# A deformable-convolution kernel on one core: output rows taken in pairs, bands of four pixels, masks copied into PSUM

## The reference, cut to what matters

```python
value = (xf @ vp_w.T + vp_b).reshape(n, L, G, cg)          # G = 8 groups of 8 channels
om = depthwise3x3(x) .reshape(n, L, c) @ om_w.T + om_b     # per group: 9 taps x (dy, dx, mask)
...
sampled = bilinear sample of value at (base + off), 4 neighbours each
out = jnp.einsum('nhwgk,nhwgkc->nhwgc', mask, sampled)
out = out.reshape(n, L, c) @ op_w.T
```

## Time and profile before

| | |
|---|---|
| median of 3 runs | 2954.0 us (2952.28 to 2957.7) |
| profiled execution | 2952.3 us, which is its span too |
| TensorE busy | 2707.7 us, 92% of the span |
| weight loads (beside it) | 2151.1 us, 73% |
| VectorE | 2190.7 us, 74% |
| ScalarE | 2106.7 us, 71% |
| GpSimd | 1925.4 us, 65% |

### The profile page before, as it was taken

The page is one execution under the profiler, slowest core; times in us unless marked ns, Lnnn a source line. Parts: engine busy times, 40 slices in busy tenths (PEclk is TensorE's granted clock), DMA queues, the critical chain, the costliest instruction groups (busy, mean ns, idle before and its releaser), DMA issues. The chain is left out here.

```text
span 2952.3 us, 99348 instructions
## 1 busy us (share of the span) xinstructions
PE 2707.7 (92%) x40456; PEld 2151.1 (73%) x40456; DVE 2190.7 (74%) x3095; ACT 2106.7 (71%) x4273; POOL 1925.4 (65%) x1451
## 2 busy tenths in 40 slices
PE   3999789993899999999999999999999999999998
PEld 2666456772677778787778777777878787777886
DVE  3555423334989898988889797989798888989763
ACT  2444256653887878787878787787878787878782
POOL 1000000003888988888888888888988888888892
PEclk8999889996899999999999999999999999999999
DMA  4555579974677777777777786777777777777675
GB/s 106 129 127 151 131 203 265 266 192 155 163 188 198 204 202 196 191 214 194 206 194 205 186 216 186 197 204 191 208 192 214 187 205 191 205 192 213 170 182 153
DMA packets 343610, 559.00 MB, mean 189 GB/s; under 512 B 159184, under 2 KB 245712, under 8 KB 342992
## 3 DMA queue, kind: packets, MB, share of 16 engines
q1 hardware_dynamic: 284112, 461.96, 62.0%
q10 hardware_dynamic: 59136, 91.76, 8.8%
HBM read 351.36 MB, written 202.19 MB: 187 GB/s over the span
## 5 line engine op out<-in xcount | busy, mean ns | idle before, releaser
L1273 PE MATMUL acc_p<-abuf,vbd 128*32 128x170 f32 (+9 forms) x20480 | 1033.8, 371 | 10.4 <-issue 9.6
L1273 PEld LDWEIGHTS acc_p<-abuf,vbd 128*32 128x32 f32 (+1 forms) x20480 | 805.1, 144 | 230.6 <-issue 24.9
L1106 ACT ACTIVATE dwt<-xp,wts 128x224 f32<-128x224 f32 x2016 | 803.3, 487 | 41.0 <-ACT wst L1130 32.3
L977 DVE TENSOR_TENSOR pr<-mh_p,ht 128x864 f32<-128x864 f32 x672 | 668.9, 1051 | 23.2
L1250 PE MATMUL win_p<-pr,smat 128*128 128x160 f32 x4032 | 617.0, 308 | 13.2 <-POOL pr L1063 12.2
L243 PE MATMUL cv<-cin,wb 128*64 128x392 bf16 x6912 | 590.1, 333 | 26.0 <-ACT cin L222 26.0
L1250 PEld LDWEIGHTS win_p<-pr,smat 128*128 128x128 f32 x4032 | 562.6, 192 | 39.1 <-issue 13.7
L243 PEld LDWEIGHTS cv<-cin,wb 128*64 128x64 bf16 x6912 | 401.7, 110 | 208.3 <-ACT cin L222 26.1
L1046 POOL TENSOR_TENSOR dwt<-dwt 128x896 f32<-128x896 f32 x224 | 519.1, 2317 | 4.7 <-ACT dwt L1106 4.7
L1060 POOL TENSOR_TENSOR pr<-pr 128x576 f32<-128x576 f32 x224 | 316.6, 1413 | 211.4 <-DVE pr L977 211.4
L967 DVE TENSOR_TENSOR mh_p<-oms,ht 128x864 f32<-128x864 f32 x224 | 392.3, 1752 | 7.1 <-ACT ht L1121 7.1
(11 more groups left out here) (131 smaller groups left out, 2579.7 us busy)
## 6 DMA issues: line engine op xcount, KB each, us to landing
abuf<-weight_scratch SPq DMA_DIRECT2D x784, 240.0 KB, 4.1
weight_scratch<-wst ACTq DMA_DIRECT2D x112, 800.0 KB, 5.1
xt<-x SPq DMA_DIRECT2D x128, 392.0 KB, 7.5
rows_scratch<-vsb SPq DMA_DIRECT2D x224, 128.0 KB, 3.2
vbd<-rows_scratch SPq DMA_DIRECT2D x896, 32.0 KB, 4.5
x_scratch<-xt SPq DMA_DIRECT2D x64, 392.0 KB, 6.7
y<-x SPq DMA_DIRECT2D x64, 392.0 KB, 5.4
x3h<-x_scratch SPq DMA_DIRECT2D x64, 392.0 KB, 5.7
```

Of the source, the lines that this page charges most:

```text
L977: dve.tensor_tensor(pr[:, j % 2, slots, :, :, :].rearrange("p k e x z -> p e k (x z)"), mh[:, a, :, :].rearrange("p (k x) z -> p k (x z)", ...
L1106: ins = act.activation(dwt[:, j % 2, k, :].rearrange("p (r w) -> p r w", w=W), image[:, r:r + BR, k % 3:k % 3 + W], ACT.Identity, scale=dw ...
L1273: mm = pe.matmul(acc_p[32 * (2 * s + b):32 * (2 * s + b) + 32, 0:2 * TN].rearrange("p (k w) -> p k w", w=W)[:, k0:k1 + 1, x0:x1], vbd[0:K, ...
```

## The change

Four things are edited. A cell grows from five to six rows of numbers (RP = 6) and its numbers are laid out so that those of two neighbouring output rows are neighbours; the contraction takes output rows in pairs (two neighbouring numbers of each cell), 48 rows of a block where it took 40, and its PSUM tile has the two rows interleaved, which `copy_acc` undoes. Bands are read for four pixels at a time: 14 reads of 16 partitions and 96 KB for 7 of 32 and 240 KB; a band as written is 960 KB for 800. `copy_weights` makes four copies of 200 numbers for two of 480 and 320. And `copy_om` is split: offsets to SBUF first in the step, masks after the products straight into the middle part of the mask products' PSUM tile; `mask_hats` multiplies the outer two parts from there (one instruction), waits, and multiplies the middle in place. `hj` is dropped, its copy goes to a part of `ht`, which ScalarE writes again later, after a wait (`far_ok`).

```diff
-PC = 2 * BR * RT * 2
+RP = RT + 1
+WP = 172
+PC = 2 * BR * RP * 2
 BAND = CT * PC
-LINE = GS * 12 * PC + PC
-SEEN = 12 * PC
+PX = 4
+SEEN = (PX + CT - 1) * PC
+LINE = GS * SEEN + PC
...
-        READS = (4, 3)
+        READS = (32 // PX, 24 // PX)
...
-                    for b in range(4 * half, 4 * half + READS[half]):
...
-                        sp.dma_start(abuf[32 * m:32 * m + 32, :, at:at + SEEN], seen).then_inc(a_in[half], 16)
+                    for m in range(READS[half]):
...
+                        sp.dma_start(abuf[GS * PX * m:GS * PX * (m + 1), :, at:at + SEEN], seen).then_inc(a_in[half], 16)
...
+                def offset_sums(i, j, to, lo, hi):
+                    return dve.tensor_tensor(
+                        to.rearrange("q w (b k g) -> q (w b) k g", b=2, g=GS),
+                        om_p[:, :].rearrange("q (k z) -> q k z", k=BR)[:, :, G * lo:G * hi].rearrange("q k (v g) -> q v k g", g=GS),
+                        ombt[:, G * lo:G * hi].rearrange("q (v g) -> q v g", g=GS).unsqueeze(2).broadcast_to(
+                            [LANES, 2 * (hi - lo), BR, GS]), ALU.add)
+                def copy_offsets(i, j):
+                    dve.wait_ge(om_ready, NT * i + j + 1)
+                    offset_sums(i, j, oms[:, j % 2, :, :], 0, 2 * TAPS).then_inc(off_ok, 1)
+                def copy_masks(i, j):
+                    t = NT * i + j
+                    dve.wait_ge(om_ready, t + 1)
+                    wait(dve, pr_ok, 3 * t)
+                    offset_sums(i, j, mh[:, 1, :, :], 2 * TAPS, 3 * TAPS).then_inc(om_ok, 1)
                 def mask_hats(i, j):
-                    wait(dve, pr_ok, 3 * (NT * i + j))
-                    dve.wait_ge(hat_ok, NT * i + j + 1)
-                    dve.tensor_tensor(mh[:, :, :, :],
-                                      oms[:, j % 2, 2 * TAPS:3 * TAPS, :].unsqueeze(1).broadcast_to([LANES, 3, TAPS, BR * G]),
-                                      ht[:, j % 2, :, 0:TAPS, :], ALU.mult).then_inc(mh_ok, 1)
+                    t = NT * i + j
+                    dve.wait_ge(om_ok, t + 1)
+                    dve.wait_ge(hat_ok, t + 1)
+                    dve.tensor_tensor(mh[:, 0:3:2, :, :], mh[:, 1, :, :].unsqueeze(1).broadcast_to([LANES, 2, TAPS, BR * G]),
+                                      ht[:, j % 2, 0:3:2, 0:TAPS, :], ALU.mult).then_inc(outer_ok, 1)
+                    dve.wait_ge(outer_ok, t + 1)
+                    dve.tensor_tensor(mh[:, 1, :, :], mh[:, 1, :, :], ht[:, j % 2, 1, 0:TAPS, :], ALU.mult).then_inc(mh_ok, 1)
...
                     if n:
-                        copy_om(*n)
+                        copy_offsets(*n)
                     n = near(i, j, 1, first, last)
                     if n:
                         mask_hats(*n)
                         products(*n)
+                    n = near(i, j, 2, first, last)
+                    if n:
+                        copy_masks(*n)
...
+                pool.memset(wst[:, :, :], 0.0)
                 pool.memset(abuf[:, :, :], 0.0).then_inc(band_clear, 1)
...
-                    act.activation(hj[:, :, :], ht[:, u, 1, :, :], ACT.Relu, bias=minus1[:, :], accum_out=far[:, bass.ts(t, 1)])
+                    act.activation(ht[:, u, 0, :, :], ht[:, u, 1, :, :], ACT.Relu, bias=minus1[:, :], accum_out=far[:, bass.ts(t, 1)]).then_inc(far_ok, 1)
                     act.activation(ht[:, u, 1, :, :], ht[:, u, 1, :, :], ACT.Identity, scale=-1.0, bias=1.0)
+                    act.wait_ge(far_ok, t + 1)
                     act.activation(ht[:, u, 0, :, :], off, ACT.Relu, scale=-1.0).then_inc(hat_ok, 1)
...
-                    for h, cells in ((0, 3), (1, 2)):
-                        m, at = RT * cells, BANK * h
+                    for k in range(BR):
+                        to = 2 * BR * (2 - 2 * (k % 2)) + BR * u + k
+                        cells = wst[:, 0, to:to + 1]
                         ins = act.activation(
...
+                            bass.AP(cells.tensor, cells.offset, [cells.ap[0], [PC, CT], [2 * BR, 2 * RT], [BAND, GS]]),
+                            win_p[:, 0:CT * WP].rearrange("p (e z) -> p e z", e=CT)[:, :, 0:RT * BR * G].rearrange(
+                                "p e (m k g) -> p e m k g", k=BR, g=GS)[:, :, :, k, :],
+                            ACT.Copy)
...
-                        k0, k1 = max(0, yq - y0 - 2), min(2 * BR - 1, yq - y0 + 2)
+                        t0, t1 = max(0, yq - y0 - 2) // 2, min(2 * BR - 1, yq - y0 + 2) // 2
...
-                                mov = bass.AP(seen.tensor, seen.offset + at, [seen.ap[0], [4 * BR + 2, n], [PC, x1 - x0]])
+                                mov = bass.AP(seen.tensor, seen.offset + at, [seen.ap[0], [8 * BR + 2, t1 - t0 + 1], [PC, x1 - x0], [1, 2]])
```

More of the change, by code:

```diff
@@ L787, in l1_pass @@
         tap_ok, dw1_ok, dw2_ok, dw3_ok, dw_ok = map(sem, ("tap_ok", "dw1_ok", "dw2_ok", "dw3_ok", "dw_ok"))
-        om_ready, om_ok, abs_ok, hat_ok, mh_ok, pr_ok, mg1_ok, mg_ok = map(sem, (
-            "om_ready", "om_ok", "abs_ok", "hat_ok", "mh_ok", "pr_ok", "mg1_ok", "mg_ok"))
+        om_ready, off_ok, om_ok, outer_ok, abs_ok, far_ok, hat_ok, mh_ok, pr_ok, mg1_ok, mg_ok = map(sem, (
+            "om_ready", "off_ok", "om_ok", "outer_ok", "abs_ok", "far_ok", "hat_ok", "mh_ok", "pr_ok", "mg1_ok", "mg_ok"))
         win_ok, wst_ok, amat_ok, accs_ok, misc_ready, misc_ok, carried, passed = map(sem, (
@@ L850, in read_weights @@
                     lines = w_d[D % 2, :]
-                    for b in range(4 * half, 4 * half + READS[half]):
-                        m = b % 4
-                        seen = bass.AP(lines.tensor, lines.offset + 8 * b * LINE, [[SEEN, 32], [XL * LINE, S], [1, SEEN]])
-                        at = (QB * half + 8 * m) * PC
-                        sp.dma_start(abuf[32 * m:32 * m + 32, :, at:at + SEEN], seen).then_inc(a_in[half], 16)
+                    for m in range(READS[half]):
+                        seen = bass.AP(lines.tensor, lines.offset + (32 * half + PX * m) * LINE,
+                                       [[SEEN, GS * PX], [XL * LINE, S], [1, SEEN]])
+                        at = (QB * half + PX * m) * PC
+                        sp.dma_start(abuf[GS * PX * m:GS * PX * (m + 1), :, at:at + SEEN], seen).then_inc(a_in[half], 16)
                 def write_values(i, j):
@@ L954, in copy_values @@
                     return ins
-                def copy_om(i, j):
-                    dve.wait_ge(om_ready, NT * i + j + 1)
[L958 to L962, removed]
@@ L1017, in _ @@
                     read_misc(j + 1, value=(0, j))
-                for j in range(2):
-                    copy_om(0, j)
+                copy_offsets(0, 0)
+                copy_masks(0, 0)
+                copy_offsets(0, 1)
                 mask_hats(0, 0)
                 products(0, 0)
+                copy_masks(0, 1)
                 for j in range(NT):
@@ L1112, in hats @@
                     t, u = NT * i + j, j % 2
-                    off = oms[:, u, 0:2 * TAPS, :]
+                    off = oms[:, u, :, :]
                     wait(act, pr_ok, 3 * (t - 1))
-                    act.wait_ge(om_ok, t + 1)
+                    act.wait_ge(off_ok, t + 1)
                     act.activation(ht[:, u, 1, :, :], off, ACT.Abs).then_inc(abs_ok, 1)
@@ L1149, in copy_acc @@
                     act.wait_ge(amat_ok, 2 * (D + 1))
-                    act.activation(accs[:, :, :].rearrange("p u f -> p (u f)"), acc_p[:, 0:2 * TN], ACT.Copy).then_inc(accs_ok, 1)
+                    act.activation(accs[:, :, :].rearrange("p u (k r w) -> p (u k) r w", r=2, w=W),
+                                   acc_p[:, 0:2 * TN].rearrange("p (t w r) -> p t r w", t=BR, r=2), ACT.Copy).then_inc(accs_ok, 1)
                 def step(i, j, first, last):
@@ L1247, in windows @@
                         terms = [(a, b) for a in range(3) for b in range(3) if 2 - (a + b - 2) == e]
-                        to = BANK * (e // 3) + 160 * (e % 3)
+                        to = WP * e
                         for n, (a, b) in enumerate(terms):
```

10 lines of the change are left out of this document (3 added, 7 removed).

## The result

| | before | after |
|---|---|---|
| median of the runs | 2953.6 us (2952.28 to 2957.7) | 2968.9 us (2964.83 to 2969.92) |
| ratio | | 1.0048, 95% interval 1.0035 to 1.0061 |
| profiled execution | 2952.3 us | 2968.0 us |
| mean of a pair, 15 pairs | 137.1 us | 137.9 us |
| mean granted clock | 0.97 | 0.95 |

What follows compares the result with a forecast made beforehand. VectorE was taken to bound steps with a half-piece sum and TensorE plain steps. From 2952.3 us, -70 for shorter steps and +33 for the clock gave 2915 profiled, 2917 median; range 2860 to 3000, the forecast's own 2880 to 2945.

Steps and rivals of the forecast that it cites:

- the ring: TensorE's next block waits for VectorE's late mask copy, and VectorE for TensorE's projection: 8.89 us a plain step.
- plain step: Step without a half-piece sum (4, 9 to 13), ending on TensorE before; forecast at 8.89 us, set by the mask-copy wait.
- rival 4: VectorE's in-place mask products in PSUM run at half rate, 0.9 us more a step: 3073 us, chance 0.06.
- sum steps: Six steps with one half-piece sum on VectorE, which waits for GpSimd's merges; forecast at 9.2 us each.
- Contraction: TensorE's matmuls reading two neighbouring numbers: 3.07 and 2.35 us forecast, from 5.28 and 4.14, at 0.94 ns a column.
- rival 3: Pairs in TensorE's contraction are read no faster, so its step takes 10.3 us: 3115 us, chance 0.10.
- rival 1: Gaps slow TensorE's clock, so every step's block runs at 1.2 GHz: 2982 us, chance 0.19.
- rival 2: ScalarE, with dearer weight copies, sets the step at 9.0 us and more: 2955 us, no difference, chance 0.10.
- 133.2 against 137.5: Forecast us for a pair of samples (14 steps) against today's: -4.3 a pair, -65 us over 15 pairs.
- steps 7 and 8: Heavy step 7 forecast at 14.1 us; step 8, which loses most by waiting for the mask copy, at 10.5.
- the clock: TensorE's half-clock stretches after longer gaps, charged in one step of three: +33 us, of 98 if in all.
- Costed at nothing: ScalarE's four copies, SP's extra reads, DMA landing times, values and loads, and GpSimd's extra memset: no time added.

Runs made afterwards that it cites:

- half_reads: The changed kernel with only the first half of the band reads, 7 for 14 in two steps, other pixels left zero: 2911.1 us, ratio 0.9863.
- spread: The changed kernel with TensorE's windows placed between two halves of the contraction, same instructions: 2943.7 us, ratio 0.9965 to the kernel before.
- spread_loads_first: The changed kernel with the contraction split around the windows, and all loads put ahead of the band reads in their step: 2935.1 us, ratio 0.9933.
- more_code: The changed kernel with 12 more matmuls of one number each behind the windows of every step: 2972.6 us, ratio 1.0077 to the kernel before.
- bands_of_8: The changed kernel with bands read for eight pixels at a time, half the reads but one and a half times the bytes: 3011.3 us, ratio 1.0201.

## Why the prediction was wrong

Right, by its own steps:
- **VectorE and the ring.** The plain step above, and the two mask products at 754 and 466 ns in place in PSUM: rival 4 falls. Of the plain steps a fifth stay under 8.88 us (8.89 forecast), of the sum steps under 9.11 (9.2).
- **Contraction.** Pairs are read faster, so rival 3 falls: 3.38 and 2.79 us for 5.28 and 4.14. They were forecast at 3.07 and 2.35; the difference of 0.4 us stays within the ring. A column took 1.04 ns (3.38 / 3264) for 1.94. The rule of the Trainium skill that was weighed there ("SBUF — State Buffer", the note on cachelines under "Door 1: The DMA port swizzle") agrees: one number of a line is dear, and two neighbours come near the rate of long runs.
- **Rivals 1 and 2.** ScalarE's copies came out at the upper bound: four of 200 take 1.68 us a step and two took 0.89. ScalarE still waits for offsets (116 us after), so it does not hold the ring. A block at half clock in every step (rival 1) is not there: the block with its projection took over 2.5 us in 30 of 215 steps after, 7 of 216 before, and the forecast had charged one in three. Stretches at 0.50 in L1 did grow, from 44 to 171 us in all. Rival 1's 2982 and rival 2's 2955 lie nearest to 2968.9 by luck: neither one's mechanism sets the steps.

Wrong: **the sum, "133.2 against 137.5", and what was added to it**. The sum set steps built from clean rows against the mean of six real pairs, which holds delays of its own. Taken alike, as the times which a fifth of each of the 14 kinds of step stay under, a pair is 135.8 us before and 133.8 after. The clean gain is then 2.0 x 15 = 30 us, not 65. Of the 35, some 25 are the mean (137.5 for 135.8) and 18 are steps 7 and 8 (14.82 and 10.97 for 14.1 and 10.5), less 8 for sum steps that came out shorter.

What a mean pair has on top of its clean steps went from 1.3 to 4.1 us: over the 15 pairs from 20 to 62, which is +42. The forecast had +33 for that and called it the clock; that the size came near is luck, as shown below. Together -30 + 42 = +12, as measured (2068.6 - 2057.1); the last pair's steps and the end of the program add 0.8 (-5 forecast) and the start 3.4. Seen as what the changed kernel takes, 15 pairs were forecast at 133.2 x 15 + 33 = 2031 us and took 2068.6. Of these 38, 9 are clean steps and 29 what real steps add.

So the links of the ring held. The sum of clean gains was too large, and two terms were missing. "Costed at nothing" speaks of ScalarE, DMA and SP, and not of TensorE's code. Steps in which a pause ended lose 40.8 us after for 7.3 before, counted as in half_reads: 34 of the 42. Steps with a half-clock stretch and no pause lose 8.7 for 6.3. In 30.5 of the 40.8 there is half clock too, so this count alone doesn't part pause and clock. spread does: it has as much time at 0.50 in L1 (177 us for 171), 3 pauses for 43, and what its steps add to the clean ones is 21 us for 62. Its time falls by only 25, as its clean steps 7 and 8 are 0.7 and 0.5 us longer.

The second missing term is the late piece in step 7 (29 us of waits), which the forecast put at nothing ("the values and the loads, as far ahead"). half_reads, which waits for no piece, has step 7 at 14.15, the forecast's 14.1. In spread_loads_first step 7 falls from 16.0 to 14.5, but the time by only 9 us, as steps 1 and 5 grew. The other half microsecond in step 8 no run explains.

Left open: why code packets start in the median 2.5 us after the block ahead of theirs is entered here, 2.0 before, and 1.2 and 1.4 in spread and more_code. Before, too, 63 of some 240 start more than 3.5 us after it, yet there are only 8 pauses; that its slower contraction hides them is argued, not shown. Whether fewer TensorE instructions for the same work would do as well as spread was not tried.

## What to carry to other kernels

Set clean steps against clean steps, and price what real steps add on top as a term of its own. When an engine's instructions get much shorter, ask whether its code still comes in time: look for idle time put down to "issue" inside a group of the same line, and number the instructions. Where one copy closes a ring, look for its earliest place between the instructions that need the buffer, not only ahead of or behind them all.

## What was not expected of the hardware

- TensorE's stops inside a line that no semaphore ended all lie at borders of 256 of its instructions: 43 after, 46 in bands_of_8, 50 in half_reads and 19 in more_code. Each ended 1.2 to 2.0 us after a 16 KB code packet had landed. With more bytes of bands in flight they lasted longer (0.99, 1.56, 2.45 us).
- The same 96 matmuls in two halves with the windows between had 3 such stops for 43.
- ScalarE's copy of 200 numbers to places that lie apart took 599 ns, one of 480 numbers 565.
